# Layer 3's feed forward as products on quarters of TensorE's array

## What is computed

```python
    def _L3_ffn_ref(x, U1, V1, b1, U2, V2, b2):
        D_MODEL, D_FF, RANK = (128, 512, 32)
        P = jnp.einsum('bsd,dr->bsr', x, U1)
        H = jax.nn.gelu(jnp.einsum('bsr,rf->bsf', P, V1) + b1)
        Q = jnp.einsum('bsf,fr->bsr', H, U2)
        return jnp.einsum('bsr,rd->bsd', Q, V2) + b2
    ...
    x = x + _L3_ffn_ref(_layernorm(x, axis=-1), L3_ffn_U1, L3_ffn_V1, L3_ffn_b1, L3_ffn_U2, L3_ffn_V2, L3_ffn_b2)
    return x
```

## Time and profile before

| | us |
|---|---|
| median of 3 runs | 1271.48 |
| lowest and highest run | 1268.71, 1274.01 |
| span of the profiled execution, from its first to its last instruction | 1270.3 |
| median less span | 1.2 |

### The profile page before, as it was taken

How to read it: one execution, slowest core, us unless ns; L and a number is a source line. 1 busy time by engine, 2 the same in 40 slices (tenths; PEclk the granted TensorE clock), 3 DMA queues, 4 the chain that set the end, 5 groups by cost and what they waited for, 6 DMA issues and landing times.

```text
span 1270.3 us, 27700 instructions
## 1 busy us (share of the span) xinstructions
PE 1149.3 (90%) x9353; PEld 829.9 (65%) x9353; DVE 697.9 (55%) x2032; ACT 613.0 (48%) x1296; POOL 380.3 (30%) x551
## 2 busy tenths in 40 slices
PE   7879999999998879999988268899999999999888
PEld 4446666878785546788865054577777667888655
DVE  5674455554554543777775163533333346777673
ACT  4542224434333433777764132534343446777663
POOL 2300002111121274455540160304040505555350
PEclk9979999999999789999999669999999999999999
DMA  8600121222220003355520301011211110111100
GB/s 251 235 1 25 38 67 32 54 52 52 62 68 1 2 1 108 103 149 145 146 68 1 50 3 42 26 50 50 61 45 56 50 55 22 31 33 29 30 3 17
DMA packets 64837, 73.53 MB, mean 58 GB/s; under 512 B 6144, under 2 KB 57392, under 8 KB 64376
## 3 DMA queue, kind: packets, MB, share of 16 engines
q1 hardware_dynamic: 61480, 64.03, 18.6%
q0 software_dynamic: 1376, 7.49, 1.8%
q10 hardware_dynamic: 1904, 0.98, 0.5%
HBM read 69.86 MB, written 0.52 MB: 55 GB/s over the span
## 4 chain that ended last, share of the span: by engine, by line
PE 77%; DVE 7%; ACT 6%; issue 4%; POOL 3%; DMA 3%; ACTq 1%; POOLq 0%; SPq 0%; DVEq 0%
PE PS L504 14%; PE PS L516 13%; PE PS L1096 8%; PE PS L791 4%; PE PS L755 4%; PE PS L1106 4%; PE PS L507 2%; PE PS L798 2%; PE PS L742 2%; PE PS L1079 2%; ACT AR L1263 2%; PE PS L1126 2%; PE PS L1086 2%; ACT XN L1263 2%; DMA AR<-AR 1%
## 5 line engine op out<-in xcount | busy, mean ns | idle before, releaser
L516 PEld LDWEIGHTS PS<-WB,AR 128*128 128x128 f32 x1568 | 189.9, 192 | 43.6 <-issue 39.5
L516 PE MATMUL PS<-WB,AR 128*128 128x128 f32 x1568 | 190.1, 275 | 0.0
L1263 ACT ACTIVATE AR<-PS,WB 128x512 f32<-128x512 f32 x160 | 110.0, 688 | 153.2 <-PE PS L504 146.7
L1096 PE MATMUL PS<-AR 128*128 128x257 f32 x512 | 138.5, 393 | 2.6 <-POOL AR L2645 2.5
L1855 DVE SCALAR_TENSOR_TENSOR ACC<-PS,SM,ACC 128x128 f32<-128x128 f32 x192 | 54.1, 344 | 95.3 <-PE PS L516 94.3
L1730 DVE TENSOR_TENSOR AR<-PS,AR 128x512 f32<-128x512 f32 (+2 forms) x71 | 49.8, 701 | 96.9 <-ACT AR L1263 40.7
L1096 PEld LDWEIGHTS PS<-AR 128*128 128x128 f32 x512 | 87.1, 190 | 22.5 <-issue 8.0
L504 PE MATMUL PS<-ZT,WB 128*128 128x512 f32 x208 | 101.0, 609 | 0.0
L504 PE MATMUL PS<-XNT,WB 128*128 128x512 f32 x168 | 86.5, 621 | 5.5 <-ACT AR L1263 5.5
L1263 ACT ACTIVATE AR<-PS 128x512 f32<-128x512 f32 (+2 forms) x83 | 43.7, 527 | 89.5 <-PE PS L507 70.9
L2589 POOL TENSOR_TENSOR AR<-AR,SM 128x516 f32<-128x516 f32 x32 | 33.8, 1055 | 155.5 <-ACT SM L1263 93.8
(11 more groups left out here) (320 smaller groups left out, 2184.7 us busy)
## 6 DMA issues: line engine op xcount, KB each, us to landing
WB<-in_units SPq DMA_DIRECT2D x49, 385.0 KB, 3.1
CTX<-in_fside SPq DMA_DIRECT2D x32, 514.0 KB, 3.9
CTX<-in_ctxT SPq DMA_DIRECT2D x96, 130.0 KB, 2.1
CTX<-in_ctxN SPq DMA_DIRECT2D x32, 129.0 KB, 2.3
CTX<-in_ctxN SPq DMA_DIRECT2D x4, 516.0 KB, 7.3
AR<-in_ctxN SPq DMA_DIRECT2D x4, 516.0 KB, 10.6
AR<-in_ctxN SPq DMA_DIRECT2D x32, 64.5 KB, 3.1
AR<-in_l1x_w POOLq DMA_DIRECT2D x1, 2048.0 KB, 8.1
```

The source lines that it names most:

```text
L516: m = pe.matmul(PS[:, 4 + hh, 128 * t:128 * t + 128], f_h[hh][:, c, 128 * t:128 * t + 128], WB[:, q, 2 * UNIT + 128 * c:2 * UNIT + 128 * c ...
L1096: m = pe.matmul(PS[:, 2 + g, 0:KEYS], x_qb[q][:, P * g:P * g + P], x_k[q], start=True, stop=True)
L1263: return act.activation(o, i, fn, **k)
```

## The change

U1 is laid four times side by side in a fourth block of VW by POOL, early in the program, so that its product holds the 32 values of P in each quarter of the partitions. V1 is loaded as four row blocks, one for each 128 hidden features, into the quarters of a new buffer V1R, and V2 is repeated in the four quarters of its place in W; SP issues these seven DMAs of 32x128 behind the loads of layer 3's units.

The first products (`rank_up`) then multiply one quarter of 32 rows of V1R by the same quarter of `f_pt`, each into a bank of its own. The second products (`rank_down`) hold 128x32 of U2 as weights and stream the hidden features, and each writes 32 partitions of a bank. The four partial sums over the hidden features stay in the four quarters, and the last product (`rank_out`), with V2 repeated, adds them up. ACC, its clearing, DVE's additions and the turning of ACC are gone. The second half of the tokens is split again into two quarters of 256 tokens for the last products, the copies and the DMAs.

Diff, without the lines that only declare or name:

```diff
@@ sync
             load_units("l3f")
+            sp.wait_ge(sig["w_l3"], 16)
+            u0, v2 = FF_UNITS["l3f"][0], SPANS["l3f_v2"][0]
+            for c in range(4):
+                r = slice(32 * c, 32 * c + 32)
+                src = units[u0 + c // 2:u0 + c // 2 + 1, 0:32, P * (c % 2):P * (c % 2) + P]
+                sp.dma_start(V1R[r, :], src.rearrange("u p n -> (u p) n")).then_inc(sig["rank_landed"], 16)
+                if c:
+                    sp.dma_start(W[r, v2:v2 + P], wpack[0:32, v2:v2 + P]).then_inc(sig["rank_landed"], 16)
 
-            for hh, ready in enumerate(("out_a", "out_d")):
-                sp.wait_ge(sig[ready], 1)
-                sp.dma_start(out[:, 4 * hh:4 * hh + 4, :], X[:, 4 * hh:4 * hh + 4, :]).then_inc(sig["out_landed"], 16)
+            for a, b, ready, k in ((0, 4, "out_d", 1), (4, 6, "out_a", 1), (6, 8, "out_d", 2)):
+                sp.wait_ge(sig[ready], k)
+                sp.dma_start(out[:, a:b, :], X[:, a:b, :]).then_inc(sig["out_landed"], 16)
@@ tensor
+            r_up = [(0, 1, 4, 5), (2, 3, 0, 1)]
-                pe.matmul(bank(2 + hh), w("l3f_u1"), XNT[:, 512 * hh:512 * hh + 512], start=True, stop=True)\
+                pe.matmul(bank(2 + hh), VW[:, 3, :], XNT[:, 512 * hh:512 * hh + 512], start=True, stop=True)\
                     .then_inc(sig["lin_ready"], 1)
+            def rank_up(hh, c):
+                r = slice(32 * c, 32 * c + 32)
+                pe.matmul(bank(r_up[hh][c]), V1R[r, :], f_pt[r, 512 * hh:512 * hh + 512], start=True, stop=True)\
+                    .then_inc(sig["up_ready"], 1)
+            def rank_down(k, c, h):
+                u2 = 2 * UNIT + P * (c % 2)
+                return pe.matmul(PS[32 * c:32 * c + 32, k, 0:h.shape[1]], WB[:, c // 2, u2:u2 + 32], h,
+                                 start=True, stop=True, skip_group_check=True)
+            def rank_out(t, k, at):
+                return pe.matmul(PS[:, k, P * at:P * at + P], ZT[:, P * t:P * t + P], w("l3f_v2"),
+                                 start=False, stop=True, skip_group_check=True)
+            pe.wait_ge(sig["rank_landed"], 16 * 7)
             hidden(0)
+            for c in range(4):
+                rank_up(0, c)
             hidden(1)
-            ff("l3f", f_pt, second=True, close=False)
+            rank_up(1, 0)
+            rank_up(1, 1)
+            pe.wait_ge(sig["h_ready"], seen.up("h_ready", 2))
+            rank_up(1, 2)
+            rank_up(1, 3)
             pe.wait_ge(sig["bias_ready"], 11)
-            carry(X)
-            turn(ACC, "down_used")
-            project(ZT, w("l3f_v2"), half_taken)
+            for k, a, n in ((6, 0, 512), (7, 512, 256)):
+                pe.matmul(PS[:, k, 0:n], ident, flat(X)[:, a:a + n], start=True, stop=False, skip_group_check=True)
+            pe.wait_ge(sig["h_ready"], seen.up("h_ready"))
+            for c in range(4):
+                if c == 3:
+                    pe.wait_ge(sig["h_ready"], seen.up("h_ready"))
+                m = rank_down(4, c, r_h[0][c])
+            m.then_inc(sig["down_ready"], 1)
+            pe.wait_ge(sig["h_ready"], seen.up("h_ready"))
+            pe.matmul(PS[:, 2, 0:256], ident, flat(X)[:, 768:1024], start=True, stop=False, skip_group_check=True)
+            pe.wait_ge(sig["down_used"], seen.up("down_used"))
+            for t in range(4):
+                m = rank_out(t, 6, t)
+            m.then_inc(sig["proj_ready"], 1)
+            for c in range(4):
+                if c:
+                    pe.wait_ge(sig["h_ready"], seen.up("h_ready"))
+                for k in range(2):
+                    m = rank_down(5 - k, c, r_h[1][c][:, 256 * k:256 * k + 256])
+                    if c == 3:
+                        m.then_inc(sig["down_ready"], 1)
+            for t, k, name in ((4, 7, "turned_a"), (6, 2, "down_used")):
+                pe.wait_ge(sig[name], seen.up(name))
+                rank_out(t, k, 0)
+                rank_out(t + 1, k, 1).then_inc(sig["proj_ready"], 1)
@@ scalar
-            ff("l3f")
-            turned(ZT[:, :])
-            act.wait_ge(sig["proj_ready"], 2 * 9 + 1)
-            act.copy(flat(X)[:, 0:512], PS[:, 6, :]).then_inc(sig["out_a"], 1)
+            for hh in range(2):
+                for c in range(4):
+                    act.wait_ge(sig["up_ready"], seen.up("up_ready"))
+                    f(r_h[hh][c], PS[:, r_up[hh][c], :], LAYERS_FF["l3f"][1],
+                      bias=WB[:, c // 2, 3 * UNIT + c % 2:3 * UNIT + c % 2 + 1]).then_inc(sig["h_ready"], 1)
+                    act.wait_ge(sig["h_ready"], seen.up("h_ready"))
+            act.wait_ge(sig["down_ready"], seen.up("down_ready", 2))
+            act.copy(ZT[:, 512:768], PS[:, 5, 0:256]).then_inc(sig["turned_a"], 1)
+            act.wait_ge(sig["proj_ready"], 2 * 9 + 2)
+            act.copy(flat(X)[:, 512:768], PS[:, 7, 0:256]).then_inc(sig["out_a"], 1)
@@ vector
-            dve.memset(flat(ACC), 0.0).then_inc(sig["dve_ran"], 1)
-            ff("l3f")
-            turned(ZT[:, :])
-            dve.wait_ge(sig["proj_ready"], seen.up("proj_ready", 2))
-            dve.tensor_copy(flat(X)[:, 512:1024], PS[:, 7, :]).then_inc(sig["out_d"], 1)
+            dve.wait_ge(sig["down_ready"], seen.up("down_ready"))
+            dve.tensor_copy(ZT[:, 0:512], PS[:, 4, :]).then_inc(sig["down_used"], 1)
+            dve.wait_ge(sig["proj_ready"], 2 * 9 + 1)
+            dve.tensor_copy(flat(X)[:, 0:512], PS[:, 6, :]).then_inc(sig["out_d"], 1)
+            dve.wait_ge(sig["down_ready"], seen.up("down_ready", 2))
+            dve.tensor_copy(ZT[:, 768:1024], PS[:, 4, 0:256]).then_inc(sig["down_used"], 1)
+            dve.wait_ge(sig["proj_ready"], 2 * 9 + 3)
+            dve.tensor_copy(flat(X)[:, 768:1024], PS[:, 2, 0:256]).then_inc(sig["out_d"], 1)
@@ gpsimd
+            pool.tensor_copy(VW[:, 3, :].rearrange("p (c r) -> p c r", c=4),
+                             w("l3f_u1")[:, 0:32].unsqueeze(1).broadcast_to([P, 4, 32])).then_inc(sig["pool_ran"], 1)
```

More of the change, by code:

```diff
@@ L145, in perceiver @@
         MK = sb("MK", [P, 3, B], I32)
-        VW = sb("VW", [P, 3, P])
+        VW = sb("VW", [P, 4, P])
+        V1R = sb("V1R", [P, P])
         PS = ctx.enter_context(nc.psum_tensor("PS", [P, 8, 512], F32))
@@ L300, in perceiver @@
         f_pt = ar(3072, TOK)
+        r_h = [[ar(4096 + 2048 * hh + 512 * c, 512) for c in range(4)] for hh in range(2)]
+        r_up = [(0, 1, 4, 5), (2, 3, 0, 1)]
         f_w = SM[:, 128:200].rearrange("p (t e) -> p t e", t=NT)
@@ L431, in _ @@
             load_units("l3f")
[L433 to L436 removed]
+            sp.wait_ge(sig["w_l3"], 16)
[9 more added lines that the diff above has]
+                sp.dma_start(out[:, a:b, :], X[:, a:b, :]).then_inc(sig["out_landed"], 16)
+            sp.wait_ge(sig["out_landed"], 48)
         @block.tensor
@@ L1244, in _ @@
                 half_taken(hh)
-                pe.matmul(bank(2 + hh), w("l3f_u1"), XNT[:, 512 * hh:512 * hh + 512], start=True, stop=True)\
+                pe.matmul(bank(2 + hh), VW[:, 3, :], XNT[:, 512 * hh:512 * hh + 512], start=True, stop=True)\
                     .then_inc(sig["lin_ready"], 1)
+            def rank_up(hh, c):
[10 more added lines that the diff above has]
+            pe.wait_ge(sig["rank_landed"], 16 * 7)
             hidden(0)
+            for c in range(4):
+                rank_up(0, c)
             hidden(1)
-            ff("l3f", f_pt, second=True, close=False)
+            rank_up(1, 0)
[3 more added lines that the diff above has]
+            rank_up(1, 3)
+            for q in range(2):
+                pe.wait_ge(sig[f"unit_landed{q}"], seen.up(f"unit_landed{q}", 16))
             pe.wait_ge(sig["bias_ready"], 11)
@@ L2574, in _ @@
             pool.wait_ge(sig["w_l3"], 16)
+            pool.tensor_copy(VW[:, 3, :].rearrange("p (c r) -> p c r", c=4),
+                             w("l3f_u1")[:, 0:32].unsqueeze(1).broadcast_to([P, 4, 32])).then_inc(sig["pool_ran"], 1)
+            seen.up("pool_ran")
             for k, of in enumerate((w("l1a_v"), w("l3a_v"), ident)):
```

11 lines of the change are left out of this document (6 added, 5 removed).

## The result

The changed kernel takes 1256.95 us (median of 4 runs, 1252.14 to 1259.41) where the kernel before takes 1271.49 beside it (4 runs, 1268.71 to 1274.01): a ratio of 0.9895, with a 95% interval of 0.9857 to 0.9933. The forecast was 1262.7 with a range of 1258.7 to 1267. So the change is faster, as forecast, and the time lies 1.75 us under the range. (Executions of the kernel before spread over some 15 us, as will be seen; four runs on each side say little about a difference of 2.)

The account below looks back on a forecast made before the run. The prediction took the last block to be bound by PE, working mostly on zeros. Its steps ended the span at 1261.5 us, 8.8 earlier, so 1271.48 - 8.8 = 1262.7 us (chance 0.50), range 1258.7 to 1267.

Parts of the forecast that it names:

- the bound from the 32x32 set: First products: four on row quarters overlap and cost 0.86 us a set, against 3.44 if none overlap.
- row quarters apart: Rival: row quarters don't overlap, column quarters do; the eight first products take 3.4 us more, 1266.1, chance 0.07.
- a fallen clock: Rival: PE at 1.2 GHz throughout the new end, its pieces double, 7.4 us more, 1270.1, chance 0.07.
- products one at a time: Rival: products on parts of the array run singly, each pass draining before the next; 1275.9 us, chance 0.02.
- The change of tiling: Switching between whole and partial array, as beside the residual: taken as 0.09 us, called a small term.
- the bound of 0.16: Most that one change of tiling costs, from the 32x32 set: 1.02 us less 2 x 0.43.
- 0.4 at most: Growth of the sum if each of six tiling changes in PE's list drains the array.
- the hold-up: Second half's second products: one waiting for its quarter delays the next quarter's first; set takes 2.15 us.
- The lower bound of the prediction: Rival: second half's quarters run side by side, 0.86 us for the set; 1261.4, chance 0.30.
- the earlier trace at 200.94: Row of the trace before: four products on four column quarters, read 1.19 us after the start, like one.
- The end: Last copy's end to span's end: 2.6 us, from 2.75 before, the halved last DMA worth 0 to 0.3.
- The runs of before scatter by 2.7 to either side of their median: Scatter used for the range: 1261.4 less 2.7 gave its lower end, 1258.7 us.

Follow-up runs that it names:

- the preamble alone: The changed kernel with the whole block of before behind the new preamble (larger buffers, POOL's copy, seven DMAs, PE's wait): 1270.83 us, ratio 0.9985 to the kernel before.
- the round robin: The changed kernel with the second half's second products written in turn over the quarters, not quarter by quarter: block 14.31 us against 14.58, one run 1259.26.
- the 30 runs above: The kernel before, unchanged, run beside the repeats of it, of the changed kernel and of the preamble alone: median 1270.55 us, from 1262.15 to 1276.31.

## Why the prediction was off, step by step

Counted from the start of ACT's copy of `f_pt`, in us (the prediction's times less 1246.16; the changed kernel's less 1242.96):

| | predicted | measured |
|---|---|---|
| first product | 0.64 | 0.73 |
| first gelu | 1.83 | 1.92 |
| third and fourth product of the second half | 3.29 | 3.38 |
| residual | 4.15 | 4.44 |
| first half's second products | 5.62 | 5.93 |
| DVE's copy of them | 6.81 | 7.13 |
| first half's last products | 7.55 | 7.87 |
| second half's second products | 8.53 | 8.96 |
| DVE's copy of 256 | 11.01 | 10.17 |
| end of the last copy | 12.70 | 12.30 |
| end of the span | 15.34 | 14.58 |

**What held.** PE bounds the block. Four products on row quarters cost little more than one: the bound from the 32x32 set was the right end, and undoing it cost 3.1. Column quarters likewise, 4.4. Eight gelus took 5.73, at the pitch of 0.72 that was read from the earlier trace rows, and were not the end of the path. SP's seven DMAs and POOL's copy cost nothing that the whole times show: the preamble alone differs by 0.1 at equal clock. PE's wait for the DMAs goes with 0.17 in that kernel's block; whether it makes the 0.09 by which the first product is late here was not tried. The clock stayed at 2.4 GHz through the block. The rivals of row quarters apart, of a fallen clock and of products one at a time fell.

**The change of tiling** was larger than the 0.09 taken. From the third and fourth product of the second half to the residual it is 1.06 where the passes are 0.86, and from the residual to the second products 1.49 where they are 1.29: some 0.2 each, above the bound of 0.16 that the prediction read. The second of these the runs take apart. With whole second products, where nothing changes behind the residual, it takes 1.39 (1247.56 to 1248.95); with whole first products, where nothing changes ahead of it, 1.39 as well (1244.58 to 1245.97). And in the kernel before, with whole products on both sides, the residual's four passes take 1.72 to the next start, no more than 4 x 0.43:

```profile
1261.63 1.88 PE L473 MATMUL PS<-X,W 128*128 128x512 f32 x4
...
1263.35 1.04 PE L452 MATMUL PS<-W,ACC 128*128 128x128 f32 x8
```

So each of the two changes beside the residual costs it 0.1. The Trainium skill, TensorEngine Tiling (Array Packing), section Key Properties, says that changing the mode drains the array. The trace agrees that a change costs something, 0.1 for each of these. The prediction's "0.4 at most" for six such changes does not follow from its own bound: six of 0.16 are 0.96, and 0.27 of that stood in the sum.

**The step that failed in size: the hold-up.** "The second product of a quarter, waiting for its quarter, holds up the next quarter's first" gave 2.15 + 0.33 to DVE's copy, 2.48; measured 1.21, and the round robin shows the same length. The lower bound of the prediction was the true one, and the earlier trace rows at 200.94 had already said that passes of different quarters interleave; I gave the order of PE's list more weight than that row. This is the term of the sum that was off most, by 1.27. The Trainium skill, TensorE: Matmul & The Clock Gate, section Part 3: Packing small matmuls, says that matmuls start and end in program order. For the starts the trace differs, and it decides: in PE's list both products of the first quarter stand ahead of the second quarter's first, but all four quarters start within some 0.05 us, while the first quarter's second product can start only 0.43 later, behind its first. For the ends the trace agrees as far as it goes: ACT's copy starts only with DVE's (1253.15 and 1253.13).

**The step that I had not seen: one queue for the two halves of 256 tokens.** Of the 1.27 gained there, 0.44 was lost again: from DVE's copy of 256 to the end of the last copy I had 1.69, and it is 2.13, because PE's list puts ACT's last products ahead of DVE's. The round robin gave it back.

**The end.** 2.28 from the last copy to the end of the span, where I took 2.6 out of 2.75.

Together: 0.43 late at the second products, 0.84 early at DVE's copy, 0.40 at the last copy, 0.76 at the end. The block gained 9.57 where the sum had 8.8. With 9.57 the forecast would have been 1261.9, inside the range and still 5 us above the measured median: what the sum had wrong does not account for the time outside the range.

**The step that put the time outside the range: the scatter.** "The runs of before scatter by 2.7 to either side of their median" came from three runs. 75 runs span 15.7 us with a standard deviation of 4.3, and the changed kernel's 11 have 3.2. Drawing three at a time from the 30 runs above and four at a time from the 11, the medians lie between 1265.2 and 1272.8 for before, and between 1256.0 and 1260.3 for the changed kernel, 8 times in 10: 3.8 and 2.2 to a side. The 1271.48 was a high draw against 1270.3 of all 75, and the 1256.95 a low one against 1258.4; both are luck of the draw. Taken as independent, 3.8 and 2.2 make 4.4 in place of 2.7, and the lower end 1261.4 - 4.4 = 1257.0, which is about where the time lies. The difference of the medians of all runs is 11.9, and that too is partly clock: 0.9597 on average for the changed kernel, 0.9583 for before, at 1 us for 0.001.

What stays open: why the clock falls at 400 to 440 us in some executions and not in others, with the same code, was not tried.

## What to carry over

A product whose contraction or result fills a quarter of the array was much cheaper on that quarter here: four of them cost little more than one, and on column quarters they took as long in either order of PE's list. The order still set when the first result could be read. What is late next is then the copies out of PSUM and the order in which PE serves two consumers that are ready together. Time a late block from an instruction that both kernels share to the end of the span: that repeated to a hundredth in the changed kernel, where the whole time scatters by some 10 us. First look at the granted clock in the block, since a stretch at the lower level that reached into it made the block of before 0.75 longer; and read the mean granted clock beside each run before a difference of medians is believed. A forecast's range takes its scatter from many runs, or, where there are three, is made wider than they are.

## What of the hardware was not expected

Two products on one quarter, standing side by side in PE's list, do not hold back the quarters behind them: sixteen passes of 256 columns in quarter order are out after 1.09 us, round robin after 1.07, though the first 256 tokens can be read only at the end of the former and 0.47 earlier in the latter. A last DMA of 128 KB rather than 256 KB ends the span 0.46 earlier. And what is the same work on the same data, but for the preamble, runs for 88.7 to 129.5 us at the lower clock level, and begins its last block up to 13.9 us apart (1236.9 to 1250.8).
